# Attention block with expert layer: late transposed loads, two-engine eviction, and a queue changed in the last stage

## The reference

```python
qkv = x @ W_qkv + b_qkv
q, k, v = jnp.split(qkv, 3, axis=-1)
scores = jnp.einsum('bqd,bkd->bqk', q, k) * inv_sqrt_d
attn = jax.nn.softmax(scores, axis=-1)
ctx = jnp.einsum('bqk,bkd->bqd', attn, v)
x = _layernorm(x + ctx @ W_out + b_out, axis=-1)
grouped = x.reshape(x.shape[:-2] + (-1, ne, d))          # groups of 16 tokens
logits = jnp.einsum('...btd,des->...btes', grouped, controller)
logits = logits + tie
perm = (logits == jnp.max(logits, axis=-3, keepdims=True)).astype(x.dtype)
sel = jnp.einsum('...btd,...btes->...besd', grouped, perm)
inner = jax.nn.relu(jnp.einsum('...besd,desf->...besf', sel, f1) + bias)
inter = jnp.einsum('...besf,esfd->...besd', inner, f2)
out = jnp.einsum('...besd,...btes->...btd', inter, perm)
x = _layernorm(x + out, axis=-1)
```

## Time and profile before

| | us |
|---|---|
| two timed runs | 2324.44 and 2468.62, median 2396.53 |
| the profiled execution | 2325.61 |
| its span, slowest core (core 4) | 2324.1 |
| spans of the 8 cores | 2295.5 to 2324.1 |
| PE busy | 1908.0 (82%) |
| DVE, ACT busy | 517.3 (22%), 556.5 (24%) |

### The profile page before, as it was taken

The page is one execution under the profiler, slowest core; times in us unless marked ns, Lnnn a source line. Parts: engine busy times, 40 slices in busy tenths (PEclk is TensorE's granted clock), DMA queues, the critical chain, the costliest instruction groups (busy, mean ns, idle before and its releaser), DMA issues.

```text
span 2324.1 us, 34078 instructions; the slowest of 8 cores (2295.5 to 2324.1 us)
## 1 busy us (share of the span) xinstructions
PE 1908.0 (82%) x13161; PEld 1301.1 (56%) x13216; DVE 517.3 (22%) x840; ACT 556.5 (24%) x1121; POOL 110.5 (5%) x209
## 2 busy tenths in 40 slices
PE   0397989899499999999999999999659687866564
PEld 0143434487377778877778777788334444442221
DVE  0011101101011110011110111101342444433555
ACT  0121223122022222222222222222044444432000
POOL 2000000000000000000000000000002020212000
PEclk9998989999799999999999999999765677565777
DMA  9814332199900100001000010000637676677997
GB/s 136 109 37 72 60 80 52 33 136 113 128 19 28 42 24 15 19 28 42 28 10 19 28 42 29 19 10 19 143 115 203 197 231 193 219 217 213 312 310 238
DMA packets 236956, 230.50 MB, mean 99 GB/s; under 512 B 147648, under 2 KB 172224, under 8 KB 235968
## 3 DMA queue, kind: packets, MB, share of 16 engines
q0 software_dynamic: 19408, 75.64, 16.8%
q10 hardware_dynamic: 108544, 83.91, 12.7%
q1 hardware_dynamic: 108848, 68.77, 12.0%
HBM read 178.06 MB, written 92.27 MB: 116 GB/s over the span
## 4 chain that ended last, share of the span: by engine, by line
PE 70%; DMA 15%; DVE 5%; issue 2%; SPq 2%; another core or an unknown queue 1%; ACT 1%; DVEq 1%; ACTq 0%; POOL 0%; POOLq 0%
PE pb L134 60%; PE pb L131 10%; DMA arenaC<-hsp 6%; DMA y<-arenaF 2%; SPq L117 2%; DMA qsp<-qstage 2%; DMA arenaA<-xbf 1%; DVE arenaF L143 1%; DVEq L143 1%; DMA arenaB<-f1b 1%; DMA xbf<-x 1%; DVE arenaA L141 1%; DMA intersp<-arenaB 1%; DVE bnbuf L143 1%
## 5 line engine op out<-in xcount | busy, mean ns | idle before, releaser
L134 PE MATMUL pb<-arenaA,arenaB 128*128 128x256 bf16 (+1 forms) x4032 | 576.9, 287 | 68.8 <-DMA arenaA<-qsp 40.6
L134 PE MATMUL pb<-arenaA 128*128 128x512 bf16 x1817 | 456.0, 384 | 128.5 <-DMA arenaA<-xbf 94.1
L134 PE MATMUL pb<-arenaA,arenaC 128*128 128x256 bf16 x4120 | 540.6, 275 | 24.6 <-DVE arenaA L141 19.0
L134 PEld LDWEIGHTS pb<-arenaA,arenaB 128*128 128x128 bf16 (+1 forms) x4032 | 412.8, 105 | 170.2 <-issue 117.7
L134 PEld LDWEIGHTS pb<-arenaA,arenaC 128*128 128x128 bf16 x4120 | 403.3, 98 | 79.2 <-issue 32.0
L141 ACT ACTIVATE arenaA<-pb,smalls 128x256 bf16<-128x256 f32 x512 | 240.7, 473 | 793.8 <-PE pb L131 761.4
L134 PEld LDWEIGHTS pb<-arenaA 128*128 128x128 bf16 x1856 | 180.2, 99 | 356.8 <-issue 167.6
L134 PE MATMUL pb<-arenaB 128*128 128x512 bf16 (+1 forms) x375 | 158.3, 508 | 83.0 <-DMA arenaC<-hsp 64.3
L143 DVE RECIPROCAL arenaF<-pb 128x256 f32<-128x256 f32 x16 | 28.1, 1758 | 883.5 <-PE pb L131 883.5
L131 PE MATMUL pb<-arenaA,arenaB 128*128 128x256 bf16 (+1 forms) x576 | 165.4, 287 | 0.0
L134 PE MATMUL pb<-arenaC 128*128 128x128 bf16 x896 | 95.3, 270 | 62.0 <-DMA arenaC<-hsp 45.4
(11 more groups left out here) (54 smaller groups left out, 921.0 us busy)
## 6 DMA issues: line engine op xcount, KB each, us to landing
intersp<-arenaB POOLq DMA_DIRECT2D x128, 256.0 KB, 3.6
arenaC<-hsp ACTq DMA_DIRECT2D x96, 256.0 KB, 4.2
arenaC<-hsp SPq DMA_DIRECT2D x64, 256.0 KB, 3.4
arenaB<-intersp SPq DMA_DIRECT2D x64, 256.0 KB, 8.9
y<-arenaF ACTq DMA_DIRECT2D x32, 512.0 KB, 9.0
xbf<-x POOLq DMA_DIRECT2D x4, 2048.0 KB, 22.3
qsp<-qstage ACTq DMA_DIRECT2D x64, 128.0 KB, 2.1
arenaA<-qsp SPq DMA_DIRECT2D x16, 512.0 KB, 3.9
```

What stands on the lines that cost most here:

```text
L134: e.matmul(o, l, r, start=st, stop=sp))
```

## The change

It has three parts.

- The early transposed loads of channels 3 to 7 are gone, with their waits; after attention each channel is loaded in one transposed DMA of 4096 tokens.
- In the selection pass of ec = 0 the last quarter (t = 24 to 31) is evicted as in the other passes, one bank by VectorE and one by ScalarE.
- In `load_it` the piece c = 2 is issued by POOL instead of ACT and counts on the semaphores of c = 3 (`ib`); the semaphores `ic` are gone. ACT's wait for the end of the expert products stands ahead of the stage instead of in `load_h5`.

```diff
-    HFCH = {3: "hf1", 4: "hf2", 5: "hf3", 6: "hfm", 7: "hf0"}
-    EHF = (NKT - 4) * 128 if NKT >= 8 else 0
...
-        if qt == NQ - 1 and EHF > 0:
-            wait("sync", "sT", kt_T[NKT - 5])
-            wait("sync", "h0", P_cnt["h0"])
-            wait("sync", "h1", P_cnt["h1"])
-            for c in range(3, NCH):
-                dma("sync", HFCH[c], B[:, c * S: c * S + EHF],
-                    hsp_d[0:EHF, c * 128:(c + 1) * 128], transpose=True)
...
-        hf_done[c] = dma("sync", hfch[c], B[:, c * S + EHF:(c + 1) * S],
-                         hsp_d[EHF:, c * 128:(c + 1) * 128], transpose=True)
+        hf_done[c] = dma("sync", hfch[c], B[:, c * S:(c + 1) * S],
+                         hsp_d[:, c * 128:(c + 1) * 128], transpose=True)
...
-            if ec == 0:
+            if ec == 0 and t < 3 * NT // 4:
...
+    wait("scalar", "sT", p4_T_done)
...
-        wait("scalar", "sT", it_free_T[slot])
         for c in range(4):
-            qn = ("sync", "sync", "scalar", "gpsimd")[c]
+            qn = "sync" if c < 2 else "gpsimd"
...
-            elif c == 2:
-                ic_ld[slot] = dma("scalar", "ic%d" % slot, dst, src_ap)
             else:
                 ib_ld[slot] = dma("gpsimd", "ib%d" % slot, dst, src_ap)
...
-        wait("scalar", "sT", max(ht2_free[hslot], p4_T_done))
+        wait("scalar", "sT", ht2_free[hslot])
...
-        wait("tensor", "ic%d" % slot, ic_ld[slot])
```

More of the change, by code:

```diff
@@ L560, in build_nc @@
     wait("sync", "h1", P_cnt["h1"])
-    hfch = HFCH
+    hfch = {3: "hf1", 4: "hf2", 5: "hf3", 6: "hfm", 7: "hf0"}
     hf_done = {}
     for c in range(3, NCH):
-        hf_done[c] = dma("sync", hfch[c], B[:, c * S + EHF:(c + 1) * S],
-                         hsp_d[EHF:, c * 128:(c + 1) * 128], transpose=True)
+        hf_done[c] = dma("sync", hfch[c], B[:, c * S:(c + 1) * S],
+                         hsp_d[:, c * 128:(c + 1) * 128], transpose=True)
     LGW = min(512, QC)
@@ L851, in build_nc @@
     ib_ld = [0, 0, 0, 0, 0]
-    ic_ld = [0, 0, 0, 0, 0]
     hld_t = [0, 0, 0, 0]
+    wait("scalar", "sT", p4_T_done)
     def pe_pt(t):
```

## The result

| | before | after |
|---|---|---|
| all executions of this comparison, median | 2328.22 us (10) | 2358.98 us (11) |
| profiled execution | 2325.61 us | 2346.23 us |
| its span, slowest core | 2324.1 us | 2344.7 us |
| ratio, 95% interval | | 1.0111, 1.0082 to 1.0139 |

The changed kernel takes 1.1% longer, some 26 us. (Both medians include executions in which one die ran at a lower clock, up to 2576 us; the ratio leaves them out.) The same kernel was timed twice more beside other runs of before: 1.0102 (1.0058 to 1.0145) and 1.0083 (1.0052 to 1.0114).

The account below looks back on a forecast made before the run. It took the chain of waits between attention and routing and, in the last stage, the full DMA engines (share 1.01) as bounds. 2325.6 + 20 - 0.5 - 2 = 2343.1 us, range 2328 to 2364.

Parts of the forecast that it names:

- case A: Whole kernel, last stage bound by full DMA engines: the summed 2343 us, +0.7%, own range 2334 to 2353; chance 0.74.
- Part 1, +20 us: Between attention and routing: late transposes lengthen the path by 20 us, ends +14 and +26.
- By bytes: Late transposes: 4.59 MB moved costs 22.7 us of DMA time, about 2 us filling gaps: +20.7 us.
- By issue: Late transposes: five issues take 24.1 us against 6.50, plus 1.5 us for the last landing: +19.1 us.
- nothing hides it: After attention: PE's first logits block needs channel 7, everything behind hangs on it, so all +20 us is on the path.
- The page's rate: Late transposes at the skill page's 261 GB/s: +15.6 us, total 4 us lower; not adopted, the kernel's 200 GB/s kept.
- Part 2, -0.5 us: Last 8 tiles of the first selection pass: VectorE takes one eviction bank, -0.5 us, ends -2.3 and +1.
- Part 3, -2 us: Last stage: 32 loads of 256 KB move from ScalarE's queue to POOL's, -2 us, ends -12.3 and +5.3.
- Nearest to the row that says full: Last stage: why -2 us was chosen, near the DMA share of 1.01, at which the steady part is worth 0.
- Case B: Last stage: ScalarE's queue is the bound, so moving loads gives -12.3 us instead of -2, total 2333; chance 0.14.
- case C: Last stage: POOL's queue becomes the bound, 54 us more at 30 us landings, 2397 us, +3.1%; chance 0.07.
- The sum: Whole kernel: profiled execution 2325.6 us plus 20, minus 0.5, minus 2, making 2343.1 us.

Follow-up runs that it names:

- four-buffer kernel: Changed kernel with four y buffers in arena A instead of two in arena F: ratio to before 1.0085, last stage 194.0 us.
- part 1 twice: Kernel before with only the early transposes replaced by one late 4096-token load per channel, run on two chips: ratios 1.0075 and 1.0094.
- part 2: Kernel before with only the last quarter of the first selection pass evicted by VectorE and ScalarE: ratio 0.999.
- part 3: Kernel before with only piece c = 2 of the last stage's loads issued by POOL: ratio 1.0011.
- parts 2 and 3 twice: Changed kernel with the early transposes given back, run on two chips: ratios to before 1.0001 and 0.9986.

## Why the prediction was right or wrong

- **Class and sign.** Within 2% was the likeliest outcome, with a rise of 17.5 us or 0.7%. Measured were 1.1% and 25.8 us (2353.0 us on the mean of the executions in the ratio, 2327.2 for before), in three comparisons 0.8 to 1.1%. All three medians lie within 2328 to 2364 us, but that range is not what its own bounds give: they make 2325.6 + 14 - 2.3 - 12.3 = 2325.0 and 2325.6 + 26 + 1 + 5.3 = 2357.9. The median of 2358.98 is inside the range and above those bounds, which is luck; the mean of 2353.0 is at the end of case A's own range.
- **Part 1, +20 us: right.** 20.5 us more to the first logits block (mean of the six profiles with late loads over 8 cores each, among them the four-buffer kernel's 38.6, 38.4; of the five without, 17.8), and alone +17.5 and +21.9 us. By bytes it was met: 205 GB/s against 200. By issue it was met in part by errors that cancel: five issues took 27.55 us and not 24.1, which makes +21.05 and not +17.6; the last landing adds 0.7 and not 1.5; and the group starts 7.4 us after the last `hsp` write instead of 8.3. That nothing hides it was right: routing behind it takes 41.6 to 41.9 us against 41.1 to 41.3, and the first selection pass and the experts are as long as before within their scatter.
- **The page's rate.** The changed kernel's transposing loads moved 205 GB/s at a share of 1.06. The 261 GB/s that the Trainium skill gives on its page "DMA: Bandwidth & Descriptors", section "Latency and other measured facts", which made 15.6 us of this term, was not reached here, and the measurement decides.
- **Part 2, -0.5 us: right as far as it can be told**, -0.3 us in the pass, which is inside the scatter.
- **Part 3, -2 us: this term was mis-sized.** This is the step of the sum that failed. Start and stage together are 206.6 us with ScalarE's queue (mean of before, part 1 twice and part 2) and 206.5 with POOL's (part 3, parts 2 and 3 twice, after three times; single profiles 205.3 to 209.0): nothing. "Nearest to the row that says full" should have been zero. The reason for the 2 us, sooner landing of `hsp` and y, did not come true at all, 9.5 us for y instead of 9.0 and 12.0 for `hsp` instead of 11.2; and where a wait for y was taken away by force, the stage kept its length.
- **Case B** fell by the four buffers, **case C** by POOL's issues of 538 ns and `intersp` landings of 8.4 us at median and 16.4 at most, under the 22 us from which it would have decided. The rule of the Trainium skill, page "SBUF — State Buffer", section "SBUF: two separate sides", by which POOL cannot write descriptors while a VectorE operation of certain kinds holds the port they share, spoke against part 3. The trace of after does not show it, with 523 to 606 ns per issue while VectorE is busy more than half the time; whether VectorE's operations in this stage are of those kinds, no run here shows.
- **The sum: its starting point failed too.** It began at the profiled execution, 2325.6 us. The cores' mean span in that profile is 2307.5 us; over 26 executions of the same kernel it is 2314.5. Its last `hsp` write came at 1639.9 us on the mean of the cores, and in all thirteen other profiles of this study at 1643.0 to 1650.7, with or without the early transposes. On the slowest core, executions of before average 2327.2 us in the comparison of the result and 2329.3 to 2333.4 in the others, so the starting point was 1.6 to 8 us too low, and the absolute time of 2343 with it; the forecast rise doesn't depend on it. With zero for part 3 and the start of its own comparison the steps give 2327.2 + 20.5 - 0.3 = 2347, against 2353.0 measured; the two repeats had means of 2359.1 and 2351.8 us, where the steps give 2354 and 2350.
- **The signs.** Two failed: the five transposes were to take 22 to 26 us (27.55), and y and `hsp` were to land sooner. The others came: PE's wait of 32.6 us in place of 10.65, selection 21.4 us later after attention's end, the same length from there to the last stage, and a last stage at a share of 0.98 that is within 8 us of before.
- **What stays open.** The three ratios of the changed kernel make +26, +24 and +19 us on the slowest core; part 1 alone makes +17.5 and +21.9, parts 2 and 3 together 0 and -3. So some 6 us of the first result are in no part alone. About 2 of them may be in the last stage: it takes 194.5 us on the mean of the five profiles that have late transposes and POOL's loads (193.1 to 196.0) and 192.7 in the three that have POOL's loads and early transposes. No run shows why, and the rest is no more than the comparisons scatter.

## What to carry to other kernels

Before a transfer is moved behind the work that covers it, ask which is the first instruction that waits for all of it, and whether it needs all of it: here one semaphore for a channel made the first block wait for 4096 tokens. With the transfers left late, quarters with a wait each took back most of the loss (1.0102 to 1.0025), and with the transfers early, a split wait and an earlier `tie` together gained 12.6 us on the kernel before. In a stage whose 16 DMA engines are full, look at their share before moving loads to another queue or adding buffers: here both changed who waits, and not how long the stage is. And one profiled execution is a poor zero for a forecast of 1%: compare the spans of all its cores with the timed runs first.

## What was not expected of the hardware

- Taking a quarter of the bytes off a queue did not shorten the landing of what stayed on it: y 9.0 to 9.5 us, `hsp` 11.2 to 12.0 us, with the DMA share at 0.98 to 1.01 in both kernels, while SP's loads of the stage, whose queue was not touched, went from 8.9 to 10.8 us.
- Twenty transposing loads of 1024 rows took 31.03 us to issue where five of 4096 took 27.55, the same bytes (31.0 to 34.3 us on the eight cores against 26.0 to 28.8).
- The same instructions take different times on the cores. In the two kernels' profiles attention's first score product comes at 445.1 to 465.3 us, and attention from there to the last `hsp` write takes 1183.3 to 1188.7 us; so most of the scatter in front of the changed code comes from the projection, and it is as large as what the edit costs.
